# A new way from the gated unit to the experts, and a new order of TensorE's work in the local layers

## The reference

```python
xn = layernorm(x)
x  = x + favor(xn) + local(xn)          # block 0
xn = layernorm(x)
x  = x + attention(xn) + experts(xn)    # block 1
# favor: 16 heads of 8, exp features (32), causal sums num / den, projection, residual, norm
# local, two layers: h = shift_token(x); q, k, v = h @ wqkv       (8 heads of 64)
#   q, k = rotary(l2norm(q) * qs), rotary(l2norm(k) * ks)
#   x = x + softmax(window of 64 back, q k^T) v @ wo
#   h = norm(shift_token(x)); a, g = split(h @ w1 + b1); x = x + (a * gelu(g)) @ w2 + b2
# attention: 16 heads of 8, full softmax over 256 keys
# experts: top 2 of 8 by xn @ Wr + rb; each (xn @ W1) * silu(xn @ W3) @ W2, weighted; one shared expert
```

## Time and profile before

| | |
|---|---|
| median of 3 runs | 2470.44 us (2469.55 to 2471.82) |
| the profiled execution | 2469.61 us, its span 2467.8 us |
| PE busy | 1954.3 us, 79% of the span |
| DVE, ACT, POOL busy | 1303.0, 731.4, 309.3 us |
| mean granted clock of PE | 0.878 |

### The profile page before, as it was taken

The page is one execution under the profiler, slowest core; times in us unless marked ns, Lnnn a source line. Parts: engine busy times, 40 slices in busy tenths (PEclk is TensorE's granted clock), DMA queues, the critical chain, the costliest instruction groups (busy, mean ns, idle before and its releaser), DMA issues.

```text
span 2467.8 us, 46598 instructions
## 1 busy us (share of the span) xinstructions
PE 1954.3 (79%) x19644; PEld 1120.4 (45%) x19644; DVE 1303.0 (53%) x3084; ACT 731.4 (30%) x1321; POOL 309.3 (13%) x242
## 2 busy tenths in 40 slices
PE   1887788778888788877888768888688877878777
PEld 1444444444454444534445435454344553445544
DVE  1555455554455554655546455555455554565544
ACT  0222242223522235122251232422233223423133
POOL 0110101102101021011110111101111102011020
PEclk9898898888988799878899789997899978989789
DMA  4000200002000020000200001000110002000010
GB/s 154 1 1 1 44 7 2 1 1 44 7 2 1 1 44 7 2 1 3 43 6 2 1 20 26 6 2 1 30 16 6 2 1 41 5 6 1 1 39 7
DMA packets 33762, 36.08 MB, mean 15 GB/s; under 512 B 3652, under 2 KB 32116, under 8 KB 33012
## 3 DMA queue, kind: packets, MB, share of 16 engines
q1 hardware_dynamic: 33556, 33.10, 6.2%
HBM read 24.44 MB, written 8.65 MB: 13 GB/s over the span
## 4 chain that ended last, share of the span: by engine, by line
PE 61%; DVE 26%; ACT 7%; issue 4%; POOL 1%; DMA 1%; SPq 1%; ACTq 0%; DVEq 0%
PE bank L831 6%; PE bank L846 5%; DVE amx L1428 5%; PE bank L935 4%; PE bank L657 4%; PE bank L856 3%; PE bank L563 3%; PE bank L691 3%; PE bank L603 3%; DVE lrec L1275 3%; DVE lmx L1261 2%; PE bank L796 2%; PE bank L678 2%; PE bank L614 2%; DVE fp L1214 2%
## 5 line engine op out<-in xcount | busy, mean ns | idle before, releaser
L1419 DVE TENSOR_TENSOR mh<-bank,silu 128x512 f32<-128x512 f32 x144 | 98.8, 690 | 232.2 <-PE bank L846 232.2
L1275 DVE RECIPROCAL lrec<-bank 128x256 f32<-128x256 f32 x64 | 112.3, 1755 | 144.0 <-PE bank L704 143.4
L441 POOL TENSOR_TENSOR lc<-lc,ls 128x512 f32<-128x512 f32 x32 | 41.0, 1280 | 1026.6 <-DVE lc L1236 1026.6
L1065 ACT ACTIVATE silu<-bank 128x512 f32<-128x512 f32 x144 | 85.1, 597 | 277.8 <-PE bank L831 277.8
L831 PE MATMUL bank<-xn2T,w_mw 128*128 128x512 f32 x288 | 164.8, 702 | 1.8
L1428 DVE TENSOR_REDUCE amx<-bank 128x2 f32<-128x512 f32 x256 | 155.0, 680 | 0.0
L603 PE MATMUL bank<-hT,w_wqkv 128*128 128x512 f32 x256 | 133.9, 666 | 23.5 <-ACT hT L967 17.3
L856 PEld LDWEIGHTS bank<-w_mw,mh 128*128 128x128 f32 x1152 | 136.7, 192 | 24.2 <-issue 24.2
L856 PE MATMUL bank<-w_mw,mh 128*128 128x128 f32 x1152 | 141.4, 277 | 0.0
L1261 DVE TENSOR_REDUCE lmx<-bank 128x4 f32<-128x512 f32 x128 | 79.5, 684 | 73.8 <-PE bank L657 73.8
L1016 ACT ACTIVATE lnmT<-bank 128x512 bf16<-128x512 bf16 x16 | 9.6, 597 | 348.2 <-PE bank L666 348.2
(11 more groups left out here) (260 smaller groups left out, 3821.9 us busy)
## 6 DMA issues: line engine op xcount, KB each, us to landing
dparts<-parts SPq DMA_DIRECT2D x8, 768.0 KB, 3.6
phi<-dparts SPq DMA_DIRECT2D x96, 64.0 KB
lc<-dparts SPq DMA_DIRECT2D x96, 64.0 KB
w_mw<-in_mw SPq DMA_DIRECT2D x3, 1152.0 KB
x_in<-in_x SPq DMA_DIRECT2D x8, 256.0 KB, 13.7
out<-res SPq DMA_DIRECT2D x8, 256.0 KB, 2.3
w_wqkv<-in_wqkv SPq DMA_DIRECT2D x1, 1536.0 KB
w_w<-in_w SPq DMA_DIRECT2D x1, 682.0 KB
```

Of the source, the lines that this page charges most:

```text
L1275: V.reciprocal(lrec[:, k % 2, :], bank_of("loc_den", k)[:, 0:SEQ]).then_inc(sem["loc_rec"], 1)
L1419: V.tensor_tensor(mh[:, n % 4, :], bank_of("moe_u", n)[:], silu[:, n % 2, :], ALU.mult).then_inc(sem["moe_h"], 1)
```

## The change

In each local layer the value matmuls go one by one between the sums; favor values move from the place behind the transposed roots (layer 1) and ahead of the gated unit's output (layer 0) to the place ahead of the transposed maxima and behind that output; the maxima are subtracted last instead of first; the output projection has a bank for each sequence. The inverse root is started from one integer step instead of two and refined by a step of second and one of third order instead of three of second order. In layer 1 the gated unit's output comes token by feature, with the residual added by identity matmuls, so `yT` goes. In the experts' part `arest` moves from GpSimd to DVE, the routing's exp moves up on ACT, gates and outputs are ordered anew, `MAX_AT` spreads the maxima over experts 3 to 7, the ring has seven banks, and `dparts` has a new layout with eight stores for one. Indentation is cut here.

```diff
...
-dparts = nc.dram_tensor("dparts", [2, 3, AH, AD, T], BF16, kind="Internal").ap()
+dparts = nc.dram_tensor("dparts", [2, 3, 2, AD, AH // 2, T], BF16, kind="Internal").ap()
...
-(0, "var"): 4, (0, "gain"): 5, (0, "gates"): 6, (1, "rT"): 7}
+(0, "var"): 4, (0, "gain"): 5, (0, "out"): 6, (1, "nmT"): 7}
...
-MAX_AT = {5: range(0, 5), 6: range(5, 10), 7: range(10, 16)}
+MAX_AT = {3: ((), (), (0, 1)), 4: ((2,), (3,), (4,)), 5: ((5,), (6,), (7,)),
+          6: ((8,), (9,), (10, 11)), 7: ((12,), (13,), (14, 15))}
...
-"five": range(0, 5), "acc": range(5, 6)}
+"five": range(0, 5), "seven": [0, 1, 2, 3, 4, 6, 7], "acc": range(5, 6)}
...
+"route_T": "seven", "moe_g": "seven", "moe_w": "seven", "moe_u": "seven", "att_max": "seven",
...
-sp.dma_start(dparts.rearrange("w s h d t -> (h d) w s t"), parts[:]).then_inc(sem["parts_out"], 16)
-sp.wait_ge(sem["parts_out"], now("parts_out", 16))
+for h in range(AH // 2):
+    sp.dma_start(dparts[:, :, :, :, h, :].rearrange("w s o d t -> (o d) (w s) t"),
+                 parts[2 * AD * h:2 * AD * h + 2 * AD].rearrange("p w s t -> p (w s) t")).then_inc(
+                     sem["parts_out"], 16)
+sp.wait_ge(sem["parts_out"], now("parts_out", 8 * 16))
...
-sp.dma_start(st_[r0:r0 + AD, :, :],
-             dparts[w_, part].rearrange("(h o) d t -> o d h t", o=2)[odd]).then_inc(
-                 sem["stack_in"], 16)
+sp.dma_start(st_[r0:r0 + AD, :, :], dparts[w_, part, odd]).then_inc(sem["stack_in"], 16)
...
-pool.wait_ge(sem["att_part1"], now("att_part1", 1))
-nc.gpsimd.tensor_tensor(arest, aqk, parts[:, :, 0, :], ALU.subtract).then_inc(sem["att_rest"], 1)
...
+values(0)
+values(1)
 sums(1)
+values(2)
 pe.wait_ge(*freed("loc_sum", l))
 pe.wait_ge(sem["loc_ss"], now("loc_ss", l + 1))
 for j in range(TT):
     last = mm(bank_of("loc_sum", l)[:, j * 16:j * 16 + 16], lsq[:, 0, j * P:(j + 1) * P],
               W["sumcol"][:], start=True, stop=True)
 last.then_inc(sem["loc_sum_ps"], 1)
+values(3)
 favor_heads(l, "sums")
...
+favor_heads(l, "nmT")
...
-favor_heads(l, "nmT")
-pe.wait_ge(sem["loc_nmT"], now("loc_nmT", l + 1))
...
+if k % 4 == 0:
+    pe.wait_ge(sem["loc_nmT"], now("loc_nmT", l + 1))
+for kt, (c0, q0, nq) in enumerate(spans):
+    for i in range(4):
+        r = slice(32 * i, 32 * i + 32)
+        ins = mm(bank_of("loc_sT", 4 * k + i)[:, c0:c0 + nq], W["nmrow"][r, g, :],
+                 lnmT[r, t + q0:t + q0 + nq], start=False, stop=True, skip_group_check=True)
+        if kt == 1:
+            ins.then_inc(sem["loc_sT_ps"], 1)
...
+    n = 2 * l + b
+    pe.wait_ge(*freed("loc_wo", n))
+    pe.wait_ge(sem["loc_o"], now("loc_o", 2 * n + 2))
     for c in range(4):
-        last = mm(o[:, t], W["wo"][:, l, c, :], loT[:, c, t], start=(c == 0), stop=(c == 3))
-last.then_inc(sem["loc_wo_ps"], 1)
+        last = mm(bank_of("loc_wo", n)[:, 0:SEQ], W["wo"][:, l, c, :],
+                  loT[:, c, b * SEQ:(b + 1) * SEQ], start=(c == 0), stop=(c == 3))
+    last.then_inc(sem["loc_wo_ps"], 1)
...
 if l == 0:
+    favor_heads(l, "mean")
...
 mm(o[:], W["mean"][:], h, start=True, stop=True).then_inc(sem["glu_mean_ps"], 1)
-favor_heads(l, "mean")
...
-favor_heads(l, "gates")
...
+for b in range(G):
+    pe.wait_ge(sem["glu_h"], now("glu_h", 6 + 2 * b))
+    last = mm(bank_of("glu_cen")[:, b * SEQ:(b + 1) * SEQ], W["center"][:], hT[:, b, 0:SEQ],
+              start=True, stop=True)
+last.then_inc(sem["glu_cen_ps"], 1)
...
+for j in range(TT):
+    mm(o[:, j * P:(j + 1) * P], xB[:, j * P:(j + 1) * P], I[:], start=(j == 0), stop=False,
+       skip_group_check=True)
+for c, (r0, m) in enumerate(HC):
+    pe.wait_ge(sem["glu_hid"], now("glu_hid", 4 + c))
+    for j in range(TT):
+        last = mm(o[:, j * P:(j + 1) * P], hid[0:m, c, j * P:(j + 1) * P],
+                  W["w2"][0:m, 1, c, :], start=False, stop=(c == 2), skip_group_check=True)
...
+if l == 0:
+    favor_heads(l, "out")
...
+expert_gate(1)
...
 expert_weight(1)
-for q in range(1, EX):
-    expert_gate(q)
+expert_gate(2)
+expert_out(0)
+expert_weight(2)
+expert_unit(1)
+for q in range(2, EX):
+    if q > 2:
+        expert_gate(q)
+    att_maxes(q, 0)
     expert_weight(q + 1)
     expert_unit(q)
-    if q not in MAX_AT:
-        expert_out(q - 1)
-        continue
-    for i, pair in enumerate(MAX_AT[q]):
-        if pair == 0:
-            pe.wait_ge(sem["stack_in"], now("stack_in", 26 * 16))
-        att_max(pair)
-        if i == 1:
-            expert_out(q - 1)
+    att_maxes(q, 1)
+    expert_out(q - 1)
+    att_maxes(q, 2)
...
-expert_gate(EX)
 expert_unit(EX)
 expert_out(EX - 1)
 expert_out(EX)
...
+for b in range(G):
+    t = slice(b * SEQ, (b + 1) * SEQ)
+    act.wait_ge(sem["loc_x"], now("loc_x", 2 * l + b + 1))
+    A(hT[0:64, b, 0:SEQ], xB[0:64, t], ACT.Copy).then_inc(sem["glu_h"], 1)
+    A(hT[64:P, b, 1:SEQ + 1], xB[64:P, t], ACT.Copy).then_inc(sem["glu_h"], 1)
...
+act.wait_ge(sem["route_d"], now("route_d", 1))
+A(rsm[:, 4:6, :], rsm[:, 2:4, :], ACT.Exp).then_inc(sem["route_exp"], 1)
 act.wait_ge(sem["att_rest"], now("att_rest", 1))
 A(parts[:, :, 1, :], arest, ACT.Copy).then_inc(sem["att_part2"], 1)
-act.wait_ge(sem["route_d"], now("route_d", 1))
-A(rsm[:, 4:6, :], rsm[:, 2:4, :], ACT.Exp).then_inc(sem["route_exp"], 1)
...
+gates(1)
+for q in range(2, EX + 1):
+    widen(q)
     gates(q)
-    widen(q + 1)
...
+if q == EX:
+    act.wait_ge(sem["att_nmT_ps"], now("att_nmT_ps", 1))
+    act.wait_ge(sem["nm_out"], prior("nm_out"))
+    A(anmT[:], bank_of("att_nmT")[0:2 * AH, 0:256].bitcast(BF16), ACT.Copy).then_inc(sem["att_nmT"], 1)
...
-link(V.tensor_scalar(t.bitcast(I32), a.bitcast(I32), 1, None, ALU.logical_shift_right))
-link(V.tensor_scalar(y.bitcast(I32), t.bitcast(I32), -1, 0x5F3759DF, ALU.mult, ALU.add))
-for i in range(3):
-    link(V.scalar_tensor_tensor(t, a, -0.5, y, ALU.mult, ALU.mult))
-    link(V.tensor_tensor(t, t, y, ALU.mult))
-    last = V.scalar_tensor_tensor(y, t, 1.5, y, ALU.add, ALU.mult)
-    if i < 2:
-        link(last)
-return last
+link(V.tensor_scalar(y.bitcast(I32), a.bitcast(I32), -0.5, 0x5F3759DF, ALU.mult, ALU.add))
+link(V.scalar_tensor_tensor(t, a, -0.1875, y, ALU.mult, ALU.mult))
+link(V.tensor_tensor(t, t, y, ALU.mult))
+link(V.scalar_tensor_tensor(y, t, 0.5625, y, ALU.add, ALU.mult))
+link(V.scalar_tensor_tensor(t, a, 64.0 / 9.0, y, ALU.mult, ALU.mult))
+link(V.tensor_tensor(t, t, y, ALU.mult))
+link(V.scalar_tensor_tensor(t, t, -10.0 / 3.0, t, ALU.add, ALU.mult))
+return V.scalar_tensor_tensor(y, t, 5.0, y, ALU.add, ALU.mult)
...
+for b in range(G):
+    n, t = 2 * l + b, slice(b * SEQ, (b + 1) * SEQ)
+    dve.wait_ge(sem["loc_wo_ps"], now("loc_wo_ps", n + 1))
+    V.tensor_tensor(xB[:, t], bank_of("loc_wo", n)[:, 0:SEQ], (xB if l else xnT)[:, t],
+                    ALU.add).then_inc(sem["loc_x"], 1)
...
-V.scalar_tensor_tensor(xB[:], bank_of("glu_out", l)[:], W["cols"][:, 12 + l:13 + l], xB[:],
-                             ALU.add, ALU.add).then_inc(sem["glu_x"], 1)
...
-dve.wait_ge(sem["yT_ps"], now("yT_ps", 1))
+    if l == 0:
+        V.scalar_tensor_tensor(xB[:], bank_of("glu_out", 0)[:], W["cols"][:, 12:13], xB[:],
+                               ALU.add, ALU.add).then_inc(sem["glu_x"], 1)
...
+V.tensor_tensor(x1[:], x1[:], bank_of("glu_out", 1)[:].rearrange("p (t d) -> p t d", t=TT), ALU.add).then_inc(sem["x1"], 1)
...
 V.tensor_tensor(rsm[:, 3, :], rsm[:, 7, :], rsm[:, 0, :], ALU.subtract).then_inc(sem["route_d"], 1)
+dve.wait_ge(sem["att_v_ps"], now("att_v_ps", 1))
+for j in range(TT):
...
+ins.then_inc(sem["att_v"], 1)
+dve.wait_ge(sem["att_part1"], now("att_part1", 1))
+V.tensor_tensor(arest, aqk, parts[:, :, 0, :], ALU.subtract).then_inc(sem["att_rest"], 1)
...
+expert_hidden(0)
+V.tensor_tensor(moe[:], x1[:], by_row(5), ALU.add).then_inc(sem["moe_base"], 1)
+
...
+for q in range(1, EX):
+    att_reduces(q, 0)
+    expert_hidden(q)
+    att_reduces(q, 1)
+    att_reduces(q, 2)
...
```

146 lines of the change are left out of this document (64 added, 82 removed).

## The result

The changed kernel takes **2387.79 us** (median of 4 runs, 2385.33 to 2401.77), the kernel before 2470.96 beside it: a ratio of 0.9681, with a 95% interval of 0.9662 to 0.9699. That is 83 us less, 10.4 us in each of eight turns. I forecast 181 us less (2289) and a range from 2205 to 2345, so the sign was right and the size was off by more than half.

What follows compares the result with a forecast made beforehand. PE's own order of work, plus its waits and reduced granted clock, was taken to bound the kernel. Terms of 22.6 us a turn, 181 in eight, taken from 2469.6 gave 2289 us, range 2205 to 2345.

Steps and rivals of the forecast that it cites:

- Values in pieces and shorter roots: Local layers: earlier square sums and a root of 8 steps instead of 11 save 2.1 and 1.8 us a turn.
- Layer 1's branch values: Layer 1: branch values moved under the maxima save 3.8 us, and 2.9 more at the score matmuls, a turn.
- the 0.62 that I asked for: Sign that the forecast holds: the granted clock of layer 1's maxima rises above 0.62.
- Bank waits in the ring of seven: Rival: bank waits in the ring of seven eat what the new order gives, same time; chance 0.02.
- the output projection's and the gated unit's 0.8 + 0.4 + 2.15: Layer 1: projection by sequence 0.8, half-wide centering 0.4, end of the gated unit 2.15 us saved a turn.
- The same loads, with the rate a fifth better: 1195.3: Experts' stacked operands land at 1195.3, PE stands 7.6 us, and 1.7 us a turn stay with the last waits.
- the last of my own signs: Load rate staying at 83 GB/s and landing past 1198 would mean a forecast too low by about 3 us a turn.
- Rival 1: Operand loads: long pieces are fast and no stall is left, 31.8 us a turn saved, 2215 us; chance 0.27.
- rival 3: Operand stores: eight small ones run one behind the other, 29 us, turn 3 us longer, 2494 us; chance 0.03.
- The estimate of 2271 by the ports: Operand loads: by the skill's port rule 1.6 MB need 14.6 us or more, the stall stays, 2271 at best.
- Layer 0, 3.6 and "this moves no end": Layer 0: branch values moved into a wait save 3.6 us a turn; branch scores ahead of the mean matmul change nothing.
- rival 2: Whole turn: the clock does not come back, short terms land at lower bounds, 2340 to 2375 us; chance 0.15.

Runs made afterwards that it cites:

- runs 1 and 2: Changed kernel with local output projections in score-ring banks: 2361.13 us; then also the ring of five started at bank 3: 2341.74 us.
- runs 3 and 6: Old single store and 1 KB loads, in the changed kernel: 2360.62 us; in it with both bank moves and maxima from expert 5: 2241.7 us.
- run 9: Changed kernel with each load's eight rows on every sixth partition instead of eight neighbours: 2350.8 us.
- run 12: Changed kernel with layer 0's branch values again behind the transposed maxima and its branch scores again behind the mean matmul: 2389.65 us.
- Run 4: Changed kernel with maxima from expert 5 on instead of 3, two pairs in a place: 2321.02 us.
- 11: Changed kernel with both bank moves, the old single store, load rows spread over the stack and maxima from expert 5 on: 2233.39 us.
- 13: Kernel 11 with layer 0's branch scores put back behind the mean matmul: 2232.6 us.

## Why the prediction was wrong, point by point

- *Values in pieces and shorter roots* held: 1.94 and 2.78 saved where I said 2.1 and 2.6 (with the clock behind the gated unit). *Layer 1's branch values* held: 6.38 against 6.7; the clock of its maxima is 0.80, above the 0.62 that I asked for.
- *"Bank waits in the ring of seven"* was the step that failed first: a term that I put at nothing. I looked for them in the new ring alone, at a chance of 0.02 and no price in the sum. One came there, 1.75 us at gate 0 in every turn, and cost nothing, since the transfer ended later. Those that cost came in the two rings whose order of banks the change shifts, 5.8 us a turn, 46 us in all (runs 1 and 2). They took the output projection's and the gated unit's 0.8 + 0.4 + 2.15 (0.35 was left) and 2.0 more at the turn's start. With its bank put right the first of these stretches saves 3.5, so those terms themselves held.
- *"The same loads, with the rate a fifth better: 1195.3"* failed next. The store was right (loads 18.7 us behind the routing product, forecast 19.2), PE's arrival too (30.5 in the fourth turn, forecast 29.5), and so was the way from the first maximum to the second attention (41.48 against 41.4). The loads took 22.6 instead of 17.9, at 66 to 74 GB/s instead of a fifth more than 83, the wait is 10.4 instead of 7.6, and routing product to second attention grew by 2.2 where I had it shrink by 1.7: 3.9 us a turn. This was the last of my own signs (a landing past 1198, priced at 3 us a turn). Longer pieces change nothing while the rows are neighbours (runs 3 and 6); what slows them is that the rows are neighbours (run 9). Why the kernel before had 83 GB/s with the same neighbours stays open. Rival 1 (long pieces are fast) was wrong for the same reason, and rival 3's serial stores did not come: 5.8 us for eight. The estimate of 2271 by the ports is not what its terms give: 14.6 us instead of 17.9 is 3.3 us a turn, so 2263.
- *Layer 0, 3.6 and "this moves no end"* failed by the clock: 1.95 saved instead of 3.6, and the scores ahead of the mean matmul cost 1.5 (run 12). The clock fell behind the shorter wait as well. This was rival 2's mechanism, in two terms, and it explains 3 of the 12 us.
- Together 5.8 + 3.9 + 1.65 + 1.5 is 12.85 where 12.3 are missing; stretches differ by some 0.5 from run to run because the half-clock stretches shift. Neither of the first two misses alone would have left my range: 2289 + 46 is 2335, 2289 + 31 is 2320.
- What I did not ask: whether the early start was worth its risk. Run 4 makes the changed kernel 67 us faster by starting two experts later.

The fastest kernel of the study (11, or 13, which is equal) takes 2233 us: 9.6% less than before and 6.5% less than the change.

## What to carry to other kernels

Where a planner hands out banks in rings, every job added or dropped rotates all banks behind it: after such a change look at each bank's last reader against its next writer, in the rings that only lose or gain a job above all. A consumer that is moved ahead of a slow transfer only turns work into a wait; find out when the operands land before deciding when to use them, and spread reductions thinly rather than early. Work moved out of a half-clock stretch was worth about its full-clock price here (1.5 us; 1.6 to 1.95 saved), since what followed it ran in that stretch instead.
